# Graph attention with residual layer norm: the bias added to the features once, the sums finished straight from their bank, and the last normalisation on ScalarE

## What is computed

```python
feats = (X @ W).reshape(-1, H, D)
a_self = jnp.einsum('nhd,hd->nh', feats, att_self)
a_neigh = jnp.einsum('nhd,hd->nh', feats, att_neigh)
scores = leaky_relu(a_self.T[:, :, None] + a_neigh.T[:, None, :], 0.2)
scores = scores + (-1e10 * (1.0 - A))[None, :, :]
attn = softmax(scores, axis=-1)
out = jnp.einsum('hij,jhd->ihd', attn, feats) + bias[None, :, :]
x = layernorm(x + relu(out.reshape(-1, H * D)))     # (x - mean) / sqrt(var + 1e-5)
```

## Time and profile before

| what | value |
|---|---|
| median of 3 runs | 821.96 us (820.8 to 823.62) |
| the profiled execution | 821.55 us |
| its span, first to last instruction | 819.7 us |
| busy: TensorE, VectorE, GpSimd, ScalarE | 72%, 74%, 62%, 10% of the span |
| bytes moved by DMA | 291.76 MB, 356 GB/s over the span |

### The profile page before, as it was taken

The page is one execution under the profiler, slowest core; times in us unless marked ns, Lnnn a source line. Parts: engine busy times, 40 slices in busy tenths (PEclk is TensorE's granted clock), DMA queues, the critical chain, the costliest instruction groups (busy, mean ns, idle before and its releaser), DMA issues.

```text
span 819.7 us, 8741 instructions
## 1 busy us (share of the span) xinstructions
PE 586.2 (72%) x2094; PEld 293.3 (36%) x2133; DVE 604.7 (74%) x1748; ACT 78.3 (10%) x355; POOL 505.3 (62%) x463
## 2 busy tenths in 40 slices
PE   2965656687769787786969776877987968783454
PEld 1711111144414344342515342543533423351333
DVE  7466997561895896867677758599887689779875
ACT  1200000120010101010010100101111010120010
POOL 1000787777727777777777777778581757575700
PEclk9966655669689979695969785978968777996778
DMA  7999999999999999999999999999999999991200
GB/s 282 361 421 363 410 397 396 397 398 398 397 411 402 392 399 401 398 399 397 398 400 397 398 398 375 333 397 399 407 397 411 407 398 406 399 393 28 50 1 26
DMA packets 67974, 291.76 MB, mean 356 GB/s; under 512 B 23062, under 2 KB 31051, under 8 KB 35152
## 3 DMA queue, kind: packets, MB, share of 16 engines
q1 hardware_dynamic: 48528, 275.40, 84.9%
q0 software_dynamic: 14208, 10.46, 4.4%
q10 hardware_dynamic: 5184, 5.31, 1.9%
HBM read 294.36 MB, written 4.75 MB: 365 GB/s over the span
## 4 chain that ended last, share of the span: by engine, by line
DMA 44%; PE 31%; DVE 17%; issue 5%; POOL 2%; ACT 0%; POOLq 0%; SPq 0%; another core or an unknown queue 0%; DVEq 0%; ACTq 0%
DMA adj_sb<-in_adj_dram 44%; PE xt_ps L666 15%; PE codes L638 11%; DVE spare L922 3%; PE ft_ps L707 2%; POOL near L434 2%; DVE near L760 1%; PE xt_ps L668 1%; PE ft_ps L623 1%; DVE val L807 1%; DVE top L908 1%; DVE z L899 1%; DVE key L868 1%; DVE z L907 1%; DVE left L870 1%
## 5 line engine op out<-in xcount | busy, mean ns | idle before, releaser
L434 POOL DMA_INDIRECT near<-node_table,idx x444 | 502.1, 1131 | 275.3 <-issue 214.4
L638 PE MATMUL codes<-adj_sb,weights 128*128 128x512 bf16 x992 | 327.3, 466 | 156.8 <-DMA adj_sb<-in_adj_dram 153.5
L638 PEld LDWEIGHTS codes<-adj_sb,weights 128*128 128x128 bf16 x1024 | 99.9, 107 | 364.2 <-issue 301.0
L666 PE MATMUL xt_ps<-spare,ident 128*128 128x360 f32 (+4 forms) x734 | 203.0, 426 | 34.7 <-DVE spare L922 34.6
L666 PEld LDWEIGHTS xt_ps<-spare,ident 128*128 128x128 f32 x734 | 139.0, 203 | 90.9 <-issue 51.7
L807 DVE MAX8 val<-codes 128x8 f32<-128x128 f32 x192 | 42.8, 285 | 110.3 <-PE codes L638 97.7
L922 DVE TENSOR_TENSOR spare<-near,spare 128x704 f32<-128x704 f32 (+12 forms) x64 | 101.3, 1644 | 7.1 <-ACT spare L561 7.1
L812 DVE MAX8 val<-codes 128x8 f32<-128x64 f32 (+2 forms) x156 | 19.6, 201 | 30.3 <-PE codes L638 29.6
L561 ACT ACTIVATE spare<-z 128x736 f32<-128x736 f32 (+10 forms) x16 | 14.9, 933 | 229.5 <-DVEq L914 229.5
L868 DVE MAX8 key<-left 128x8 f32<-128x168 f32 (+2 forms) x79 | 28.5, 361 | 2.2
L631 PE MATMUL codes<-place,weights 128*128 128x512 bf16 x58 | 28.7, 495 | 0.3 <-issue 0.2
(11 more groups left out here) (160 smaller groups left out, 475.7 us busy)
## 6 DMA issues: line engine op xcount, KB each, us to landing
adj_sb<-in_adj_dram SPq DMA_DIRECT2D x256, 1024.0 KB, 16.9
near<-node_table,idx POOLq DMA_INDIRECT x444
node_table<-spare ACTq DMA_DIRECT2D x4, 648.0 KB, 9.7
spare<-in_x_dram SPq DMA_DIRECT2D x4, 512.0 KB, 7.4
self_sb<-node_table ACTq DMA_DIRECT2D x16, 121.5 KB, 7.5
x_sb<-in_x_dram SPq DMA_DIRECT2D x4, 384.0 KB, 18.3
out_dram<-x_sb SPq DMA_DIRECT2D x1, 768.0 KB, 15.9
self_sb<-node_table ACTq DMA_DIRECT2D x16, 40.5 KB, 10.0
```

What stands on the lines that cost most here:

```text
L434: pool.indirect_dma_start(out=near[:, near_at(t) + k, :], out_offset=None, in_=table[:, :], in_offset=bass.IndirectOffsetOnAxis(ap=idx[t % ...
L638: last = pe.matmul(codes[i][:, :], weights[:, kk, :], adj_bf[q][:, k * GC:(k + 1) * GC, 1], start=False, stop=(kk == BITS - 1))
L666: last = pe.matmul(to[:, a:b, :], ident[:, :], slot_rows(t, s, a, b), start=(s == 0), stop=(s == W - 1))
```

## The change

Four things are changed.

1. The bias is added once to the projected features. `bias_sb` is now 80 columns wide (16 zeros, then the 64 of the bias); `take_feats` adds it while it moves the features out of their bank. Its load moves from behind `x_r` to behind `att_self`, and VectorE's first wait covers five parameter loads, not four.
2. `finish` takes the three ordinary rows of a tile directly from the bank: a reciprocal of their denominators and a multiplication, both reading the bank. Only the fourth row, which is added up from pieces, still goes through `sums`. The bias addition, the copy of the sums and the copy of mean and variance are gone. The bank is handed back (`sums_read`) after the multiplication.
3. The normalisation is one ScalarE activation for each block of 128 rows, x * rstd + (-mean * rstd), 64 blocks in all. VectorE only makes the two factors (`scale`).
4. Turn 2 (tiles 12 to 14) gets its factors before `finish(15)`, and ScalarE takes roots and normalises turn by turn. Turn 0 is normalised on ScalarE behind `flag_codes(12)`, turn 1 ahead of `exps(14)`.

```diff
+            sp.dma_start(bias_sb[:, 2 * H:PC], flat(bias, P)).then_inc(params_loaded, 16)
             x_rows = x.rearrange("(p j) f -> p j f", j=J)
...
                         sp.dma_start(x_r[:, :], x[0:R, :]).then_inc(d_loaded, 16)
-                        sp.dma_start(bias_sb[:, :], flat(bias, P)).then_inc(bias_loaded, 16)
...
+            def normalise(c):
+                wait_apart(act, scale_ready, c + 1)
+                for part in parts_out(c):
+                    for b in range(part.start, part.stop):
+                        ins = act.activation(x_sb[:, b, :], x_sb[:, b, :], ACT.Identity, bias=stats[:, b, 0:1], scale=rstd[:, b:b + 1])
+                ins.then_inc(out_ready, 1)
...
-            for c, (a, b) in enumerate(TURNS_OUT):
-                if b + 1 >= NT:
-                    take_root(c)
+            for c in (len(TURNS_OUT) - 2, len(TURNS_OUT) - 1):
+                take_root(c)
+                normalise(c)
...
-            dve.wait_ge(params_loaded, 64)
+
+            step(dve.memset(bias_sb[:, 0:2 * H], 0.0))
+            dve.wait_ge(params_loaded, 80)
...
-                dve.tensor_copy(nodes[:, g * GB:(g + 1) * GB, 0:PC], fv).then_inc(feats_copied, 1)
+                dve.tensor_tensor(nodes[:, g * GB:(g + 1) * GB, 0:PC], fv, bias_sb[:, :].unsqueeze(1).to_broadcast([P, GB, PC]),
+                                  ALU.add).then_inc(feats_copied, 1)
...
-                dve.tensor_copy(sums[:, 0:REST, :], sums_ps[t % 2][:, 0:REST * SC].rearrange("p (r c) -> p r c", c=SC))
-                step(dve.tensor_reduce(sums[:, REST, :], sums_ps[t % 2][:, REST * SC:(REST + K) * SC].rearrange("p (k c) -> p c k", c=SC), AX.X, ALU.add))
+                ps = sums_ps[t % 2][:, 0:(REST + K) * SC].rearrange("p (r c) -> p r c", c=SC)
+                dve.reciprocal(rden[:, 0:REST, :], ps[:, 0:REST, 0:H])
+                step(dve.tensor_reduce(sums[:, REST, :], ps[:, REST:REST + K, :].rearrange("p k c -> p c k"), AX.X, ALU.add))
+                step(dve.reciprocal(rden[:, REST, :], sums[:, REST, 0:H]))
...
                 dve.sem_inc(sums_read, 1)
-                step(dve.reciprocal(rden[:, :, :], sums[:, :, 0:H]))
...
-                step(dve.tensor_tensor(att[:, :, :], att[:, :, :], bias_sb[:, :].unsqueeze(1).to_broadcast([P, RING, F]), ALU.add))
...
-                    ins = dve.bn_aggr(mv[:, i, :], bn6[:, i, :])
-                step(ins)
-                for o, blocks in parts:
-                    ins = dve.tensor_copy(stats[:, blocks, :], mv[:, o, :])
+                    ins = dve.bn_aggr(stats[:, block_at(t, i), :], bn6[:, rank(i), :])
                 step(ins)
...
-            def normalise(c):
+            def scale(c):
+
                 wait_apart(dve, std_ready, c + 1)
                 for part in parts_out(c):
                     ins = dve.reciprocal(rstd[:, part], std[:, part])
                 step(ins)
                 for part in parts_out(c):
-                    full = [P, part.stop - part.start, F]
-                    ins = dve.tensor_tensor(x_sb[:, part, :], x_sb[:, part, :], stats[:, part, 0].unsqueeze(2).to_broadcast(full), ALU.subtract)
+                    ins = dve.scalar_tensor_tensor(stats[:, part, 0], stats[:, part, 0], -1.0, rstd[:, part], ALU.mult, ALU.mult)
...
                 if n == sum_at(NT - 1):
                     find_over()
+                    scale(len(TURNS_OUT) - 2)
```

More of the change, by code:

```diff
@@ L149, in gat_resnorm @@
         self_key = sb("self_key", [P, NT, 8], fp32)
-        bias_sb = sb("bias_sb", [P, F], fp32)
+        bias_sb = sb("bias_sb", [P, PC], fp32)
         ident = sb("ident", [P, P], fp32)
@@ L184, in gat_resnorm @@
         scrap = sb("scrap", [P, C_MAX + 2 * RING * QUARTERS], fp32)
+        pow_f = scrap[:, 0:BITS]
+        one_i, bit_i, pow_i = (scrap[:, k * BITS:(k + 1) * BITS].bitcast(i32) for k in range(1, 4))
         scrap_m = sb("scrap_m", [P, Z_MAX + T_MAX], fp32)
@@ L303, in gat_resnorm @@
         std_ready = sem("std_ready")
+        scale_ready = sem("scale_ready")
         out_ready = sem("out_ready")
@@ L582, in _ @@
                     flag_codes(t)
+                    last_n = n - RING
+                    for c, (a, b) in enumerate(TURNS_OUT):
+                        if c < len(TURNS_OUT) - 2 and last_n <= finish_at(b) < n:
+                            normalise(c)
             count_slots(NT - 1)
             for n in range(STEPS, ATTEND[NT - 1] + 1):
+                for c, (a, b) in enumerate(TURNS_OUT):
+                    if c < len(TURNS_OUT) - 2 and finish_at(b) >= STEPS - 1 and n == max(finish_at(b), STEPS):
+                        normalise(c)
                 attention(n)
-            for c, (a, b) in enumerate(TURNS_OUT):
-                if b + 1 >= NT:
-                    take_root(c)
+            for c in (len(TURNS_OUT) - 2, len(TURNS_OUT) - 1):
+                take_root(c)
+                normalise(c)
             act.wait_ge(stored, 32 * len(TURNS_OUT))
@@ L929, in finish @@
                 wait_apart(dve, slots_summed, t + 1)
[L930 to L937 removed]
+                ps = sums_ps[t % 2][:, 0:(REST + K) * SC].rearrange("p (r c) -> p r c", c=SC)
+                dve.reciprocal(rden[:, 0:REST, :], ps[:, 0:REST, 0:H])
+                step(dve.tensor_reduce(sums[:, REST, :], ps[:, REST:REST + K, :].rearrange("p k c -> p c k"), AX.X, ALU.add))
+                step(dve.reciprocal(rden[:, REST, :], sums[:, REST, 0:H]))
+                for o, of in ((slice(0, REST), ps[:, 0:REST, H:SC]), (slice(REST, RING), sums[:, REST:RING, H:SC])):
+                    ins = dve.tensor_tensor(att[:, o, :].rearrange("p i (h d) -> p i h d", d=D), of.rearrange("p i (h d) -> p i h d", d=D),
+                                            rden[:, o, :].unsqueeze(3).to_broadcast([P, o.stop - o.start, H, D]), ALU.mult)
+                step(ins)
+                dve.sem_inc(sums_read, 1)
                 parts = ((slice(0, REST), slice(NH + REST * t, NH + REST * t + REST)), (slice(REST, RING), slice(t, t + 1)))
@@ L989, in dense_finish @@
                 wait_apart(dve, d_rows, n + 1)
-                step(dve.tensor_tensor(datt, drow_ps, bias_sb[0:R, :], ALU.add))
-                step(dve.scalar_tensor_tensor(dy[:, :], datt, 0.0, x_r[:, :], ALU.max, ALU.add))
+                step(dve.scalar_tensor_tensor(dy[:, :], drow_ps, 0.0, x_r[:, :], ALU.max, ALU.add))
                 step(dve.bn_stats(dbn6[:, :], dy[:, :]))
@@ L1011, in normalise @@
                 for part in parts_out(c):
-                    full = [P, part.stop - part.start, F]
-                    ins = dve.tensor_tensor(x_sb[:, part, :], x_sb[:, part, :], stats[:, part, 0].unsqueeze(2).to_broadcast(full), ALU.subtract)
+                    ins = dve.scalar_tensor_tensor(stats[:, part, 0], stats[:, part, 0], -1.0, rstd[:, part], ALU.mult, ALU.mult)
                 step(ins)
-                for part in parts_out(c):
-                    full = [P, part.stop - part.start, F]
-                    ins = dve.tensor_tensor(x_sb[:, part, :], x_sb[:, part, :], rstd[:, part].unsqueeze(2).to_broadcast(full), ALU.mult)
-                step(ins)
-                dve.sem_inc(out_ready, 1)
+                dve.sem_inc(scale_ready, 1)
             def keep_dense():
@@ L1057, in attentions @@
                                 add_eps(c)
-                            if u == b:
-                                normalise(c)
+                            if u == b and c < len(TURNS_OUT) - 2:
+                                scale(c)
                 for u in range(NT):
@@ L1088, in _ @@
                     find_over()
+                    scale(len(TURNS_OUT) - 2)
                 clear()
                 attentions(n)
-            normalise(len(TURNS_OUT) - 1)
+            scale(len(TURNS_OUT) - 1)
             dve.wait_ge(groups_summed, 1)
```

11 lines of the change are left out of this document (removed).

## The result

The changed kernel takes **818.78 us** (median of 6 runs, 818.2 to 820.39) against 821.38 us for the kernel before in the same runs (820.52 to 823.62). The ratio is 0.9961 with a 95% interval of 0.9942 to 0.998: faster by 0.39%, just over the 0.3% that can be told from no change. The forecast was 818.4 us in a range of 815.9 to 820.8. The profiled execution took 818.96 us, its span 817.1 us; before, 821.55 and 819.7.

What follows compares the result with a forecast made beforehand. The adjacency stream was taken to bound the kernel up to about 738 us, then a single chain to the end. 821.55 - 2.58 (end stage) - 0.6 (front) = 818.4 us, range 815.9 to 820.8.

Steps and rivals of the forecast that it cites:

- What bounds the kernel: Up to about 738 us the adjacency stream sets the time, save for two holes; VectorE's savings beside it are worth nothing.
- The finish: In finish(15), cheaper reciprocal step, one multiplication split, bias addition and copy of mean and variance gone: -0.94 us.
- Turn 2 out of the way: Normalising tiles 12 to 14 no longer stands between finish(15) and the epsilon of turn 3: -2.52 us.
- Turn 3 on ScalarE: Last normalisation: two small steps, hand-over and four activations take 2.16 us against 1.28 on VectorE: +0.88 us.
- The upper bound: Turn 3's four activations at 0.46 us each, 0.36 apart, end after 1.54 us, judged by line 492.
- Turns 0 and 1 on ScalarE: Their 32 and 16 blocks take 11.6 and 5.9 us; exps(14) signals 1.3 us late, but this is covered: cost 0.
- The rival of ScalarE's queue: Turn 1's activations ahead of exps(14) hold VectorE back; at 0.9 us each the kernel takes 825.3 us; chance 0.05.
- The front: Start of the stream: without the bias load ahead of it, quarter 7 goes out earlier; -0.6 us, between -1.7 and +1.1.
- The rival in which the front gives nothing: The bias broadcast ahead of x delays the whole stream by 1.1 us, giving 820.1 us; chance 0.20.
- The hole at 505: Dip in the stream at 505 to 525 us, about 4.6 us lost; expected unchanged, counted 0.
- The stores follow as before: Output stores behind the last normalisation were expected unchanged, those of turn 2 some 6 us earlier.
- the end stage: From finish(15) through the last normalisation: -0.94 - 2.52 + 0.88 = -2.58 us, between -3.5 and -2.3.

## Why the prediction was right

*What bounds the kernel.* This held. VectorE's busy time fell by 23 us in all (604.7 to 581.7), and putting the passes back on it changed nothing. What moved the time were the hole in front, the stretch from 806 us on, and the last store.

*The finish*, forecast at -0.94: it measured 4.05 to 2.96, **-1.09 us**. By its terms, from start to start: the copy and the sum of the pieces, left unchanged in the forecast, went from 0.74 to 0.50, since the reciprocal of 24 (0.31) is shorter than the copy of 216 (0.38), and the sum behind it too; the reciprocal step from 0.39 to 0.24 (0.27 forecast); the multiplications from 0.46 to 0.64 (0.52 forecast); and the bias and the copy of mean and variance are gone with 0.46 and 0.42. Part of what the first of these terms won and the last but one lost is one and the same: the handing back of the bank (`sums_read`) stood behind the sum of the pieces, and now stands behind the multiplications. The gap behind its place moved with it, from 0.14 us behind the sum (the row below ends at 808.72, the next begins at 808.86) to 0.15 behind the multiplications (807.97 to 808.12). The multiplications themselves took 0.49 (807.48 to 807.97), which is what was counted for these two shapes, so the reading of the bank cost nothing here. No run takes the finish by itself; its 1.09 us is read from the rows.

```profile
808.42 0.30 DVE L931 TENSOR_REDUCE sums<-xt_ps 128x72 f32<-128x144 f32 x1
```

*Turn 2 out of the way*, forecast at -2.52: right. The pass is gone from the row order, and the move by itself gave 2.5 us (2.0 by the medians).

*Turn 3 on ScalarE*, forecast at +0.88: 810.46 to 812.56 is 2.10 us, against 1.28 before, **+0.82**. The four activations took 1.43 where 1.54 was counted, at 0.426 us each:

```profile
L542 ACT ACTIVATE x_sb<-x_sb,stats,var 128x64 f32<-128x64 f32 x64 | 21.6, 426 | 8.1 <-DVEq L1026 8.1
```

The upper bound, from the one row with an operand per partition, was the right one to take. An estimate from the figures of the Trainium skill, "ScalarE: Activation LUTs", section "What ACT_TABLE_LOAD costs", is 425 ns and 332 apart for this form; the row has 426, and twelve in 4.09 us are 0.333 apart. The section "Rules for kernel authors" on the same page of the Trainium skill has simple adds and multiplications on VectorE, and here the runs agree: four operations on VectorE did the same work in 0.98 us.

*Turns 0 and 1 on ScalarE*, forecast at 0: right, and by its own cover. The sixteen activations took 5.41 us and `attend(14)` waited 1.77 us for them (1.3 were forecast); tripling them showed that 6.2 us are covered and the rest is paid. The rival of ScalarE's queue had this mechanism right; its price per activation was not reached.

*The front*, forecast at -0.6 between -1.7 and +1.1: the sign was right, the step was wrong, and the sign of being wrong that the prediction had named, quarter 7 out after 33, came (34.04). It said that quarter 7 would go out 0.6 us earlier, near 32.4 us, since SP no longer issues the bias ahead of it. Over the eight profiles with the load at its new place it went out at 32.35 to 34.04, 33.4 in the mean; over the two with the old place, at 33.05 and 33.73, 33.4 as well. The issue saved went into the block of `x_r`, 21.19 and 22.06 us long with the old order and 22.5 in the mean with the new one. What gave 1.2 us by the ratio (0.2 to 2.4) and 1.3 us in the last packs was the other term, which the text counted for its lower end alone: the broadcast itself had been in the way of quarter 7, and two microseconds of the stream behind it ran at 41 and 117 GB/s. The rival in which the front gives nothing falls by the single move.

*The hole at 505*, forecast at 0: right (306 against 308 GB/s).

*What was missing.* "The stores follow as before" was wrong by **1.5 us**. The prediction had seen that the final flags would run beside the activations, and counted nothing for what follows them. With turn 3 on ScalarE the flag is computed beside the activations, 0.5 us ahead of their end, and the instruction load that comes about 2 us behind the flag meets the last store. Before, the flag came 1.1 us behind the last pass, at 817.83, and no instruction load stands in the profile from 816 us to its end at 819.7; the store had landed by then. The Trainium skill, "Runtime: NRT & Kernel Launch", section "Instruction fetch mechanics", says that instruction memory is refilled in blocks of 16 KiB by a DMA queue of the sequencer, and that a branch out of the present window makes such a fetch; the size and the place behind the branch agree with this trace. The Trainium skill, "DMA: Bandwidth & Descriptors", section "Queues, rings and completion order", has each engine change between queues at whole packets only. The 0.9 us that one packet held one engine is what this looks like here.

So the end stage was forecast rightly, and that the whole sum came out near the time was in part luck, by two misses of opposite sign: -1.09 - 2.52 + 0.82 = -2.79 at the end, -1.3 in front, +1.5 at the last store make -2.6; forecast were -2.58 at the end and -0.6 in front, -3.2 in all. One bound was off: by its own terms the end stage with slow reads of the bank is -0.74 - 2.52 + 0.88 = -2.38, not -2.3, which takes 0.1 us off the upper end of the range.

What stays open is the size of the front in a single run. With the same order of issues the block of `x_r` lasted 21.4 to 21.7 us in three of the eight profiles and 22.8 to 23.2 in five; in the three, the hole was nearly closed (385 to 391 GB/s in 30 to 40 us), and their last packs, 738.47 to 738.80, are earlier than those of the five, 738.99 to 739.82. What sets this from run to run was not found, and the runs of one kernel lie 1.4 to 5.2 us apart.

## What to carry to other kernels

Ask of each edit what it does to the order, ahead of what it does to the engines: two moved statements gave here what the whole change gave, and work that was taken off VectorE beside the stream was worth nothing that could be measured. Follow the chain past the last operation to the last store's landing, and look there for what a flag or a branch now starts earlier. A small transfer in a hole of a stream can cost more than its issue, as here, and more bytes moved early are no gain until the end of the stream is seen to move: filling the hole with the load in pieces did not move it.

## What the runs showed of the hardware

- One 16 KB instruction load held one DMA engine for 0.9 us and delayed the landing of a 32 KB store from 1.6 us to between 3.1 and 3.3. Moving the flag behind the last operation, or the branch behind the store, brings 1.6 back.
- A strided load of 512 KB in small pieces blocks the next issue on its queue for 21 to 23 us; cut in four with quarters between, the longest of their issues took 4.27 us:

```profile
30.40 0.34 SPq L393 DMA_DIRECT2D adj_sb<-in_adj_dram  x1
...
34.66 4.27 SPq L388 DMA_DIRECT2D z<-in_adj_dram  x1
```

- Four `tensor_scalar` of 64 columns with two operands per partition take 0.98 us on VectorE, four activations of the same form 1.43 us on ScalarE.
